# Masked attention on one core: q projected with the product of Wq and Wk, x's own parts in place of k

## The reference

```python
q = x @ Wq.T + bq;  k = x @ Wk.T + bk;  v = x @ Wv.T + bv     # x: 4096 x 128
scores = where(adj > 0, q @ k.T / sqrt(128), -9e15)           # adj: 4096 x 4096, int32
y = x + elu(softmax(scores) @ v)
out = (y - mean(y)) / sqrt(var(y) + 1e-5)                     # of each row
```

## Time and profile before

| | |
|---|---|
| median of three runs | 434.64 us |
| the profiled execution | 434.69 us, span 432.9 us |
| PE busy | 422.1 us (98%) |
| DVE busy | 364.0 us (84%) |
| ACT busy | 354.9 us (82%) |
| POOL busy | 343.6 us (79%) |
| granted TensorE clock | 0.996 of full speed |

### The profile page before, as it was taken

The page is one execution under the profiler, slowest core; times in us unless marked ns, Lnnn a source line. Parts: engine busy times, 40 slices in busy tenths (PEclk is TensorE's granted clock), DMA queues, the critical chain, the costliest instruction groups (busy, mean ns, idle before and its releaser), DMA issues.

```text
span 432.9 us, 11401 instructions
## 1 busy us (share of the span) xinstructions
PE 422.1 (98%) x3479; PEld 311.0 (72%) x3479; DVE 364.0 (84%) x671; ACT 354.9 (82%) x737; POOL 343.6 (79%) x613
## 2 busy tenths in 40 slices
PE   8999899999999999999999999999999999999994
PEld 6564577777777777777777777777777777777783
DVE  1788898888889898888889888888899988888783
ACT  4779878888888888888888988888888988888892
POOL 0065558889888988898888888898889888898874
PEclk9999999999999999999999999999999999999998
DMA  8934999999999999999999999999999999999550
GB/s 225 380 109 125 262 268 229 264 228 267 279 276 277 264 248 264 277 265 257 251 279 262 262 242 279 266 259 252 270 267 264 247 263 282 261 256 229 103 104 20
DMA packets 149932, 104.76 MB, mean 242 GB/s; under 512 B 133024, under 2 KB 141728, under 8 KB 141728
## 3 DMA queue, kind: packets, MB, share of 16 engines
q1 hardware_dynamic: 149488, 104.41, 91.5%
q10 hardware_dynamic: 432, 0.20, 0.2%
HBM read 69.47 MB, written 2.10 MB: 165 GB/s over the span
## 4 chain that ended last, share of the span: by engine, by line
POOL 58%; issue 18%; PE 17%; ACT 3%; DVE 2%; POOLq 2%; ACTq 0%; DVEq 0%
POOL p_rows L322 25%; POOL res L336 6%; POOL rstd L360 4%; POOL neg_mean L347 3%; POOL y L341 3%; POOL att_sum L329 3%; POOL var L356 3%; POOL att L331 3%; PE ps_out L819 3%; POOL centred L349 2%; POOL expm L338 2%; POOL var_eps L358 2%; PE ps_t L720 2%; PE ps_scores L780 2%; PE ps_scores L781 2%
## 5 line engine op out<-in xcount | busy, mean ns | idle before, releaser
L322 POOL TENSOR_TENSOR p_rows<-scores,p_rows 128x256 f16<-128x256 f32 x252 | 175.9, 728 | 8.3 <-ACT p_rows L470 8.3
L591 DVE CUSTOM_DVE_ANT_0 scores<-ps_scores,adj 128x1024 f32<-128x1024 f32 x128 | 156.0, 1219 | 14.5 <-issue 11.1
L453 ACT ACTIVATE scores<-scores,neg_max 128x1024 f32<-128x1024 f32 x128 | 145.7, 1138 | 2.3 <-DVE neg_max L600 2.3
L606 DVE TENSOR_TENSOR p_lo<-ps_t,p_hi 128x512 f16<-128x512 f32 x124 | 82.6, 685 | 27.9 <-ACT p_hi L462 27.5
L577 DVE TENSOR_SCALAR adj<-adj 128x1024 f32<-128x1024 int32 x128 | 104.9, 820 | 0.0
L780 PE MATMUL ps_scores<-k_hi,q_hi 128*128 128x512 f16 x256 | 97.1, 379 | 0.1
L781 PE MATMUL ps_scores<-k_lo,q_hi 128*128 128x512 f16 x256 | 97.0, 379 | 0.0
L782 PE MATMUL ps_scores<-k_hi,q_lo 128*128 128x512 f16 x256 | 97.0, 379 | 0.0
L819 PE MATMUL ps_out<-v_parts,p_hi 128*128 128x256 f16 x496 | 95.3, 273 | 0.7 <-DVE p_lo L606 0.7
L819 PE MATMUL ps_out<-v_parts,p_turned 128*128 128x256 f16 x496 | 95.0, 273 | 0.0
L821 PE MATMUL ps_out<-v_parts,p_lo 128*128 128x128 f16 x496 | 88.5, 219 | 0.0
(11 more groups left out here) (92 smaller groups left out, 474.3 us busy)
## 6 DMA issues: line engine op xcount, KB each, us to landing
adj<-in_adj_dram SPq DMA_DIRECT2D x64, 1024.0 KB, 5.3
out_dram<-y_out SPq DMA_DIRECT2D x32, 64.0 KB, 5.0
x_rows<-in_x_dram SPq DMA_DIRECT2D x4, 256.0 KB, 4.0
x_rows<-in_x_dram SPq DMA_DIRECT2D x2, 512.0 KB, 6.0
p_turned<-p_rows SPq DMA_TRANSPOSE x63, 4.5
w_rows<-in_L_gnn_Wq_dram ACTq DMA_DIRECT2D x1, 64.0 KB, 2.5
w_rows<-in_L_gnn_Wk_dram ACTq DMA_DIRECT2D x1, 64.0 KB, 3.2
w_rows<-in_L_gnn_Wv_dram ACTq DMA_DIRECT2D x1, 64.0 KB, 3.8
```

What stands on the lines that cost most here:

```text
L322: last = nc.gpsimd.tensor_tensor(p_rows[c][:, w:][:, cols], s_sb[s][:, c * PIECE:c * PIECE + w][:, cols], p_rows[c][:, 0:w][:, cols], ALU. ...
L453: nc.scalar.activation(s_sb[s][:, cols], s_sb[s][:, cols], ACT.Exp, bias=neg_max[:, s:s + 1], accum_out=p_sums[:, s, c:c + 1]).then_inc(ex ...
L591: nc.vector.tensor_tensor_reduce(out=s_sb[s][:, cols], in0=ps_scores[c % 2][:, :], in1=mask_sb[s][:, cols], scale=SCALE, scalar=-3.0e38, o ...
L606: nc.vector.tensor_tensor(p_lo[:, k, :], ps_t[bank_of(s, g)][:, :], p_hi[:, k, :], ALU.subtract).then_inc(plo_ready, 1)
```

## The change

- PE multiplies Wq and Wk once (`FOLD`), and Wk with bq (`FOLD_B`). q is projected with this product. k is not projected: ACT takes the high part of the transposed x (`high_of_k`), DVE its low part (`low_of_k`), and the scores are q by x.
- bk gives each query row a constant. PE makes its weights (`ROW`, `ROW_B`) from bk spread over 128 columns (`bk_wide`). POOL multiplies x by them, 512 rows at a time (`row_terms`), and DVE sums (`row_sums`), each in eight pieces. The constant goes into the row maximum: it is subtracted and added back, and the smaller of the result and the value without it is the bias of exp. This makes the row maximum four operations of DVE where it was two.
- The transposes of x go to the accumulators ps_t and ps_out in place of ps_scores. The copies of x of groups 1 to 3 move from ACT to DVE. The transposes of groups 6 and 7 and the v groups 0 and 1 come after the scores of step 3 of the first row. The v groups, the masks of rows 0 and 1 and DVE's loop are placed anew; periods 2 to 5 of DVE are written out ahead of its loop.

The diff, cut to its core:

```diff
-V_AT = range(2, 2 + STEPS)
+V_FIRST = 2
+V_AT = {2: 3, 3: 4, 4: 5, 5: 6, 6: 7, 7: 8}
+X_BY_DVE = (1, 2, 3)
+X_FIRST = 6
...
+        ps_four = ps_t + ps_out
+
         def ps_xt(g):
-            return ps_scores[g // 2 % 2][:, g % 2 * BANK:(g % 2 + 1) * BANK]
...
+        ps_fold = ps_scores[1]
+        FOLD, FOLD_B, WV, ROW, ROW_B = (slice(a, b) for a, b in ((0, D), (D, D + 1), (BANK, BANK + D), (2 * D, 3 * D),
+                                                              (3 * D, 3 * D + 1)))
+
+        def ps_q(g):
+            return ps_scores[0][:, BANK:PIECE] if g == 0 else ps_t[g % 2][:, :]
...
+        def wait_x_free(engine, g):
+
+            wait_x_copied(engine, g)
+            engine.wait_ge(k_lo_made, g + 1)
...
+            def row_terms(g):
+
+                rows = slice(g * BLOCKS, (g + 1) * BLOCKS)
+                pool.wait_ge(row_copied, 2)
+                wait_x_in(pool, g)
+                if g >= 2:
+                    pool.wait_ge(row_done, 2 * g - 2)
+                nc.gpsimd.tensor_tensor(row_prod[:, g % 2], x_rows[:, rows, :],
+                                        row_w[:, :].rearrange("p (a d) -> p a d", a=1).to_broadcast([P, BLOCKS, D]),
+                                        ALU.mult).then_inc(row_multiplied, 1)
+
+            for g in (0, 1):
+                row_terms(g)
...
             period(1, 1, has_end=False)
+            for g in (2, 3):
+                row_terms(g)
             period(2, 0, has_end=False)
+            for g in (4, 5):
+                row_terms(g)
             pool.wait_ge(bv_in, 16)
             period(3, 1, first=True)
+            for g in (6, 7):
+                row_terms(g)
             period(4, 0, first=True)
             period(5, 1)
...
+            def high_of_k(g):
+                act.wait_ge(xt_ready, g + 1)
+                nc.scalar.activation(k_hi[:, g * BANK:(g + 1) * BANK], ps_xt(g), ACT.Copy).then_inc(k_hi_made, 1)
+
+            def high_of_q(g):
+                act.wait_ge(proj_ready, g + 1)
+                act.wait_ge(fold_copied, 2)
+                nc.scalar.activation(q_hi[:, g * BANK:(g + 1) * BANK], ps_q(g), ACT.Identity, bias=bq_k[:, 0:1]).then_inc(proj_hi, 1)
...
             copy_x(0)
-            act.wait_ge(wt_ready, 1)
-            nc.scalar.activation(w_t[:, 0:2, :], ps_t[0][:, 0:2 * D].rearrange("p (n d) -> p n d", d=D), ACT.Copy).then_inc(wt_copied, 1)
-            copy_x(1)
-            act.wait_ge(b_in, 16 * 2)
-            high_of_projection(0)
-            for g in range(2, STEPS + 2):
-                if g < STEPS:
-                    copy_x(g)
-                if g == 2:
-                    act.wait_ge(wvt_ready, 1)
-                    nc.scalar.activation(w_t[:, 2, :], ps_out[0][:, 0:D], ACT.Copy).then_inc(wvt_copied, 1)
-                high_of_projection(g - 1)
+            high_of_k(0)
+            high_of_k(1)
+            high_of_q(0)
+            high_of_k(2)
+            high_of_k(3)
+            act.wait_ge(wvt_ready, 1)
+            nc.scalar.activation(wv_t[:, :], ps_fold[:, WV], ACT.Copy).then_inc(wvt_copied, 1)
+            for g in range(4, STEPS):
+                if g >= X_FIRST:
+                    copy_v(g - X_FIRST)
+                copy_x(g)
+                high_of_k(g)
...
+            def low_of_q(g):
                 cols = slice(g * BANK, (g + 1) * BANK)
-                dve.wait_ge(proj_hi, n + 1)
...
+                nc.vector.scalar_tensor_tensor(out=q_lo[:, cols], in0=ps_q(g), scalar=bq_k[:, 0:1],
+                                               in1=q_hi[:, cols], op0=ALU.add, op1=ALU.subtract).then_inc(proj_lo, 1)
+
+            def row_sums(g):
+
+                rows = slice(g * BLOCKS, (g + 1) * BLOCKS)
+                dve.wait_ge(row_multiplied, g + 1)
+                nc.vector.tensor_reduce(row_raw[:, rows], row_prod[:, g % 2], AX_X, ALU.add).then_inc(row_done, 1)
+                dve.wait_ge(row_done, 2 * g + 1)
+                nc.vector.tensor_scalar(row_bias[:, rows], row_raw[:, rows], row_b[:, 0:1], None, ALU.add).then_inc(row_done, 1)
...
+            def low_of_k(g):
+                cols = slice(g * BANK, (g + 1) * BANK)
+                dve.wait_ge(k_hi_made, g + 1)
+                nc.vector.tensor_tensor(k_lo[:, cols], ps_xt(g), k_hi[:, cols], ALU.subtract).then_inc(k_lo_made, 1)
+
+            def copy_x(g):
+                dve.wait_ge(xt_ready, g + 1)
+                nc.vector.tensor_copy(x_t[:, g * BANK:(g + 1) * BANK], ps_xt(g)).then_inc(xt_copied_dve, 1)
...
                 dve.wait_ge(max_found, i + 1)
-                nc.vector.tensor_scalar(neg_max[:, s:s + 1], max_raw[:, s:s + 1], LOG_P_SCALE, None,
-                                        ALU.add).then_inc(max_ready, 1)
+                nc.vector.tensor_scalar(max_log[:, s:s + 1], max_raw[:, s:s + 1], LOG_P_SCALE, None,
+                                        ALU.add).then_inc(log_added, 1)
+                dve.wait_ge(log_added, i + 1)
+                dve.wait_ge(row_done, 2 * (i // BLOCKS + 1) if isinstance(i, int) else 2 * STEPS)
+                nc.vector.tensor_tensor(max_full[:, s:s + 1], max_log[:, s:s + 1], row_bias[:, bass.ds(i, 1)],
+                                        ALU.subtract).then_inc(full_found, 1)
+                dve.wait_ge(full_found, i + 1)
+                nc.vector.scalar_tensor_tensor(out=neg_max[:, s:s + 1], in0=row_bias[:, bass.ds(i, 1)], scalar=max_full[:, s:s + 1],
+                                               in1=max_log[:, s:s + 1], op0=ALU.add, op1=ALU.min).then_inc(max_ready, 1)
...
+                    if has_scores and not warm and p == 0 and j in (1, 3):
+                        low_of_k(X_FIRST + j // 2)
+                    if has_scores and not warm and p == 0:
+                        for c in ((1,), (2, 3), (), ())[j // 2] if j % 2 == 1 else ():
+                            mask_piece(0, 0, c)
+                        for c in ((), (), (0,), (1, 2))[j // 2] if j % 2 == 1 else ():
+                            mask_piece(1, 1, c)
...
+                    if j in rows_at:
+                        row_sums(rows_at[j])
...
+            dve.wait_ge(b_in, 16 * 2)
+            nc.vector.tensor_copy(bk_wide[:, :], b_cols[:, 1:2].to_broadcast([P, P])).then_inc(wide_set, 1)
+            dve.wait_ge(fold_ready, 1)
+            nc.vector.tensor_copy(w_qk[:, :], ps_fold[:, FOLD]).then_inc(fold_copied, 1)
+            nc.vector.tensor_copy(bq_k[:, 0:1], ps_fold[:, FOLD_B]).then_inc(fold_copied, 1)
+            low_of_k(0)
+            low_of_k(1)
+            low_of_q(0)
+            copy_x(1)
+            low_of_k(2)
+            copy_x(2)
+            low_of_k(3)
+            dve.wait_ge(row_ready, 1)
+            nc.vector.tensor_scalar(row_w[:, :], ps_fold[:, ROW], SCALE, None, ALU.mult).then_inc(row_copied, 1)
+            nc.vector.tensor_scalar(row_b[:, 0:1], ps_fold[:, ROW_B], SCALE, None, ALU.mult).then_inc(row_copied, 1)
+            copy_x(3)
+            for g in range(4, X_FIRST):
+                low_of_k(g)
+            mask_piece(0, 0, 0)
+            period(0, 0, has_1=False, has_2=False, warm=False, rows_at={5: 0})
+            period(1, 1, has_2=False, warm=False, rows_at={4: 1})
+            for p in range(2, 6):
+                period(p, p % 2, rows_at={2: {2: 2, 6: 3}, 3: {2: 4, 6: 5}, 4: {2: 6, 6: 7}}.get(p, {}))
...
+            def project_q(g):
+                if g == 0:
+                    pe.wait_ge(fold_copied, 1)
+                elif g < 3:
+                    wait_x_free(pe, 6 + g % 2)
+                else:
+                    pe.wait_ge(proj_lo, g - 1)
+                wait_x_copied(pe, g)
+                nc.tensor.matmul(ps_q(g), w_qk[:, :], x_t[:, g * BANK:(g + 1) * BANK],
                                  start=True, stop=True).then_inc(proj_ready, 1)
...
                 if g < 2:
-                    pe.wait_ge(proj_lo, last_user(2 + g))
+                    wait_x_free(pe, 2 + g)
+                    pe.wait_ge(wvt_copied, 1)
...
             def transpose_x(g):
-                for n, (begin, end) in enumerate(X_CHUNKS):
-                    if g == begin:
-                        pe.wait_ge(x_in[n], 16)
+                wait_x_in(pe, g)
                 if g >= 4:
-                    pe.wait_ge(xt_copied, g - 3)
+                    wait_x_free(pe, g % 2 if g < 6 else g - 2)
...
-            for n in range(2):
-                last = nc.tensor.transpose(ps_t[0][:, n * D:(n + 1) * D], w_rows[:, n, :], ident[:, :])
-            last.then_inc(wt_ready, 1)
+            nc.tensor.matmul(ps_fold[:, FOLD], w_rows[:, 0, :], w_rows[:, 1, :], start=True, stop=True)
+            pe.wait_ge(b_in, 16 * 2)
+            nc.tensor.matmul(ps_fold[:, FOLD_B], w_rows[:, 1, :], b_cols[:, 0:1], start=True, stop=True).then_inc(fold_ready, 1)
             transpose_x(1)
-            pe.wait_ge(wt_copied, 1)
-            pe.wait_ge(xt_copied, 1)
-            project(0)
-            project(1)
+            project_q(0)
+            transpose_x(2)
```

(39 more changed lines are left out.)

96 lines of the change are left out of this document (44 added, 52 removed).

## The result

The changed kernel takes 450.74 us (median of 4 runs, 449.17 to 451.68) against 434.65 for the kernel before on the same chip: a ratio of 1.037 (95% interval 1.034 to 1.040), **16.1 us slower**. The forecast was 439.9, the range ended at 445.0. The profiled execution took 450.75 us with a span of 449.0.

What follows compares the result with a forecast made beforehand. The prediction took PE, 98% busy, to be paced by DVE's p_lo of group 5 through a two-row loop. From 434.69 us, -3.3 + 2.3 + 0.9 + 4.9 + 0.4 = +5.2 gave 439.9 us; range 432.5 to 445.0.

Steps and rivals of the forecast that it cites:

- The start: Before the steady rows: eight k projections go, 6.9 us of PE time, partly given back to waits; -3.3 us, bounds -1.3 and -6.9.
- followed through the queues so, the fourth masking of row 0 starts at 26.7: Start of the kernel: that masking comes at 26.7 instead of 29.72, giving a lead of 3.3 us at row 2.
- The steady part: Rows 4 to 30: DVE's two added operations after the maximum cost 0.19 us a row over 26 rows, +4.9 us; ends 0 and 9.9.
- the way round over two rows: Dependency loop through PE, ACT, POOL and DVE: spans two rows and pays the 0.38 us once, so 0.19 a row.
- 13.97 + 10.49 = 24.46: Row k's group 6 transposes to row k+1's product, then to the next such transposes: 24.46 us, 12.23 a row, the measured pace.
- 2 x 0.19 = 0.38: DVE between maximum and p_lo of group 5: two more dependent operations, 0.19 us apart, add 0.38 us without idle time.
- every row pays in full: Rival for the steady rows: ACT or POOL passes the stall on, 9.9 us instead of 4.9, total 444.9; chance 0.12.
- cover: Rival: DVE's 0.85 us wait before p_lo of group 4 absorbs the added work, only the start counts; 431.8 us, chance 0.20.
- The row terms: Rows 0 to 4: POOL's eight products and DVE's sums for bk's constant cost +2.3 and +0.9 us; bounds 0 and 4.0.
- DVE's load and POOL's lateness: Rows 2 to 4: DVE's work of 12.96 us a row sets the pace, +2.3; POOL's products delay att_sum, +0.9.
- The end: End of the kernel: ACT stands waiting for the last neg_max and nothing covers the added operations; +0.4 us.
- The parts' own bounds: Slowest limit of each term: start -1.3, row terms 4.0, steady rows 9.9, end 0.4 us.

Runs made afterwards that it cites:

- e1: The changed kernel without bk's row constant: no row products, sums or their weights, and the old two-operation row maximum; 433.68 us, ratio 0.9965.
- e2: e1 with the changed kernel's four-operation row maximum, on a row constant set to zero; 442.08 us, ratio 1.016.
- e3: The changed kernel with the old two-operation row maximum; the row constants are made but not used; 435.55 us, ratio 1.0017.
- e9: The changed kernel with max_full and neg_max written with one tensor operand and column scalars; 449.68 us, ratio 1.0359.
- e10: The changed kernel with each POOL product of 128x512 made in four of 128x128; 446.33 us, ratio 1.027.
- e15: The changed kernel, nothing left out, with only the start reordered as in e11; 450.39 us, ratio 1.0359.
- e11: e1 with PE's bias product moved behind the second transposes and first q projection, which fill the wait for bk; 433.39 us, ratio 0.9975.
- e6: The changed kernel with the third piece's mask moved in DVE's queue from ahead of p_lo of group 5 to behind it; 443.72 us, ratio 1.0205.
- e8: e1 with the loads of bq and bk issued behind the first x transfer instead of the third; 434.14 us, ratio 0.9994.
- e5: The kernel before with two more dependent one-column additions of zero between row maximum and neg_max; 440.82 us, ratio 1.014.
- e4: The kernel before with four more dependent one-column additions of zero between row maximum and neg_max; 449.60 us, ratio 1.0335.
- e16: The changed kernel, nothing left out, with the start of e15, POOL's products in pieces (e10) and the mask moved (e6); 439.48 us, ratio 1.0129.
- e7: The kernel before with the third piece's mask moved in DVE's queue to behind p_lo of group 5; 433.54 us, ratio 0.9976.

## Why the prediction was wrong

**The bill.** Alone, the parts cost -1.1 (e1), +8.4 (e2 over e1) and +1.9 (e3 over e1), together +9.2. The change costs 16.1, so 6.9 us are in no part alone. In the profiled executions two places hold them. Up to row 1 after is 1.8 us behind e1; e9 and e10, which hold all that after does, are at e1's place there, and the difference is PE's clock in the start (below). Rows 2 to 4 take 44.57 us where the parts give 39.9 (39.0 of e3 and 3 x 0.28), so 4.7 come of the meeting; in e15 it is 6.4.

**The start (-3.3, measured -1.1 in e1 and +0.9 in after).** The step that failed is "followed through the queues so, the fourth masking of row 0 starts at 26.7": it starts at 30.27 in after, 28.51 in e1 and 27.13 in e11. Two things were missing in the chain.

The first is PE's pace. In every trace PE is at half pace from its first transposes of x (1.06 to 1.12 us for four, before included) and goes over to full pace at one moment. The view by windows shows 1.00 at the start only because it has no record of the clock there. The trace's first record, of full clock, begins at 5.79 us in before, 13.40 in after, 10.79 in e1 and 10.99 in e6, and at 5.37 to 5.88 in e2, e3, e9 and e10, and the durations change at these moments. So the start of after ran at PE's lower level for 7.6 us longer than that of before. e9 has the same order of instructions and the same wait, and behind the wait it was at full pace (PE's timeline of e9):

```profile
6.99 0.38 PE L856 MATMUL ps_scores<-b_cols,w_rows 128*128 128x1 f32 x2 [1.33 <-DMA b_cols<-in_L_gnn_bk_dram]
7.24 0.63 PE L844 MATMUL ps_t<-ident,x_rows 128*128 128x128 f32 x4
7.76 1.12 PE L822 MATMUL ps_scores<-x_t,w_qk 128*128 128x512 f32 x2
```

Row 1 is at 46.63 in after, and at 44.63 and 44.70 in e9 and e10. The lower level therefore costs about 2 us, in one execution and not in others of the same order. (In e6 row 1 is at 46.74, but there the wait for bk was 1.92 us as well.) The forecast gave the wait for bk 1.3 us, and it took 1.08; the pace had no term at all.

The second thing is missing at full pace too: e9 and e10 lead by 1.1 us at row 1, not by some 3. The text had the first mask of row 0 at 14.5 and the first masking at 15.2. In e10 they start at 15.12 and 16.07, and the mask waits for the first rows of adj:

```profile
15.12 0.73 DVE L641 TENSOR_SCALAR adj<-adj 128x1024 f32<-128x1024 int32 x1 [0.22 <-DMA adj<-in_adj_dram]
```

In e11, whose queues are earlier, DVE waits 1.08 us for that load, and e8 waits 1.74. The text named the load as a limit and then did not use it. In e8 x's own transfer (1.01 us of PE) and the low part of the last k stand close behind as well.

**The steady part (+4.9, measured +6.9).** The mechanism was right: the way round over two rows, so that half of each delay counts. The sum 13.97 + 10.49 = 24.46 was no evidence for it, since both terms contain the measured pace and any two points give twice 12.23. e5 put it to the test with the 0.38 of the forecast: 0.18 a row, forecast 0.19. The step that failed is the term "2 x 0.19 = 0.38": it took for three different instructions the spacing of one kind. In the loop max_full starts 0.28 behind max_log (0.19 in rows that are written out: 91.39 and 91.58 in row 4), the three-operand form is 0.22 long, and the mask starts 0.14 behind it and not 0.07. That is 0.55, half of it 0.27, and 12.23 + 0.27 = 12.50, as measured. The Trainium skill ("Perfetto Trace Analysis", "Optimizing Scalar/DVE Operations") puts the overhead of a DVE operation at about 60 ns; by that rule the two would be 0.12, and the runs go further away from it than the trace of before did. The rival "every row pays in full" is refuted by e5 and e2 (12.41 and 12.51, not 12.61 and 12.78), with e4 as a warning that half is not a law. The rival "cover" is refuted by the same paces. DVE's wait ahead of p_lo of group 4 did shrink, from 23.6 to 14.6 us between 70 and 400 us, but its wait ahead of a masking pass grew from 10.1 to 15.6.

**The row terms (+2.3 and +0.9, together +3.2; measured +7.9).** Apart from each other the parts give the size that was forecast: rows 2 to 4 take 2.4 us more in e3 than in e1 and 0.9 more in e2, together 3.3. How it divides between DVE's load and POOL's lateness is not shown. A row sum with its addition took 1.18 us in most of these rows and not 0.78 (the addition 0.56, not 0.19). What failed is that the two parts were costed each beside the kernel of before and added. The products of POOL were looked at for what they delay in POOL's queue; that they would lie beside the only stretch of DVE without idle time, the one to which this same change adds two operations, was not asked. The row for it was quoted in a rival: res took 0.90 beside a mask of 1.11. The Trainium skill ("SBUF — State Buffer", "SBUF: two separate sides") speaks of a lock for the whole instruction that also meets DVE operations with two inputs in SBUF. The trace agrees down to a single column: 1.18 and 1.22 us beside products of 1.24, 0.38 to 0.41 beside those of 128x128 (e10), no block of these operations where the second input is a column scalar (e9), though the mask behind them was blocked instead.

**From a block to 4.7 us.** One blocked operation in row 1 and two in row 3 delay p_lo by 1.0 and 2.0 us; PE idles 2.12 and 3.11 us. Behind such a stall the granted clock fell to 0.50 for 3.4 us: behind 2.12 in after, 2.63 in e6, 2.13 and 3.11 in e15. That is an estimated 1.7 us each time. It leaves 3.0 of the 4.7 in after, and 3.0 of the 6.4 in e15, which is the delay of p_lo in full: 1.0 and 2.0. The profiled executions of e9, e10 and e16, with stalls of at most 2.06, 1.67 and 1.02, show no such stretch from 44 to 90 us, nor did every long stall bring it (79.84 in after). The record of the other executions points the same way: the changed kernel's four took 449.17, 450.75, 450.73 and 451.68 us at mean granted clocks of 0.995, 0.994, 0.988 and 0.987, and e9's slowest took 451.40 at 0.991 where the others took 449.0 to 450.3 at 0.998 and 0.999. No run set the clock on purpose, so it is not shown that the stall is what brings the fall.

**The end (+0.4, measured +0.4).**

**Range and chances.** Slower at 0.69 was right. The upper end, 445.0, is the rival in which every row pays in full, with all other terms at their forecast. The parts' own bounds together (-1.3, 4.0, 9.9, 0.4) would have reached 447.7, and the measured 450.74 lies above that too: no case had an interaction.

**What stays open.** What decides when PE's clock rises at the start, and at which stall it falls later, was not controlled. Why rows 2 to 4 take 1.1 us more in e10 (40.96) than the parts give (39.9), and the rest of the difference between e10's 446.33 and the 443.9 of the parts, was not traced.

## What to carry to other kernels

Two parts of a change that are cheap beside the kernel before can be dear beside each other: lay the new instructions of all engines over each other before adding the terms up, first where the critical engine has no idle time. A small operation added to a stretch without slack is costed by the instructions that it puts there, form by form, and multiplied by the share of the round trip that it is in; here half, up to 0.55 us, since the way round took two rows. If a dependent chain must stand there, move independent work behind what is waited for (e6, e7), and cut the other engine's long instructions in pieces (e10). If one form of an operation is blocked, changing the form can pass the wait on to the next instruction (e9): look at the whole stretch, not at the operation.

## What the hardware showed

- An operation on one column with two tensor inputs took 1.18 to 1.22 us on DVE beside a product of 128x512 on POOL, instead of 0.16 to 0.22; with scalar operands it was not blocked (0.21 and 0.27), but the mask of 128x1024 behind it was (1.49 and 1.31, where 0.68 is usual).
- More POOL work gave a faster kernel: products in pieces cost POOL 1.3 to 1.5 us a pair, and the kernel's median was 4.4 us less.
- Behind idle times of 2.12 to 3.11 us PE's granted clock was at 0.50 for 3.4 us, in some executions and at some of the stalls.
- From its first transposes PE ran at its lower level (1.06 us for what took 0.60 later) until 5.4 to 13.4 us, while the view of the clock, which has no record there, shows 1.00.
- Dependent operations of the same short form started 0.19 us apart on DVE; in the loop a two-tensor form that takes its column by a register started 0.28 behind.
